# Joining the stages of a three-stage attention kernel early, loading its shifted rows in 112 and 15 partitions, and storing from ScalarE's queue

## What is computed

```python
xn = layernorm(x)                       # x: (16, 512, 128), 16 batches
x = x + causal_attention(xn) + transformer(xn)
# causal_attention: 16 heads of 64, with a relative bias
# transformer, DEPTH = 2 layers, 8 heads of 64, window 64, HID = 341:
h = shift_token(x)                      # columns 64..127 come from the token before
q, k, v = split(h @ wqkv); q, k = rotary(l2norm(q) * qs, l2norm(k) * ksc)
x = x + local_attention(q, k, v) @ wo
h = layernorm(shift_token(x)) * lg + lb
a, g = split(h @ w1 + b1)
x = x + (a * gelu(g)) @ w2 + b2
```

## Time and profile before

| what | us |
|---|---|
| median of 3 runs (2702.74 to 2705.8) | 2703.7 |
| the profiled execution | 2707.02 |
| its span, first to last instruction | 2705.2 |
| causal attention, then 20 us of loading | to 1315.5 |
| local attention, layer 0 / 1 | 1339.0 to 1865.7 / 2018.0 to 2541.8 |
| gated MLP, layer 0 / 1 | 1865.7 to 2010.2 / 2541.8 to 2685.7 |
| sum and store | 2685.7 to 2705.2 |
| PE / ACT / DVE / POOL busy, share of the span | 94% / 80% / 74% / 60% |

### The profile page before, as it was taken

The page is one execution under the profiler, slowest core; times in us unless marked ns, Lnnn a source line. Parts: engine busy times, 40 slices in busy tenths (PEclk is TensorE's granted clock), DMA queues, the critical chain, the costliest instruction groups (busy, mean ns, idle before and its releaser), DMA issues. The chain is left out here.

```text
span 2705.2 us, 71234 instructions
## 1 busy us (share of the span) xinstructions
PE 2547.8 (94%) x24208; PEld 1988.1 (73%) x24208; DVE 2009.4 (74%) x5647; ACT 2158.3 (80%) x6335; POOL 1629.7 (60%) x1947
## 2 busy tenths in 40 slices
PE   7999999999999999999599999997979999999796
PEld 4777777777777777777378888885767888888575
DVE  4666666666666666666389999995659999999565
ACT  5888888888888888888389999996438999999642
POOL 3444444444444444444389999994229999999521
PEclk8999999999999999999799999998989999999898
DMA  2000000000000000000311111111111111111112
GB/s 72 7 7 10 9 9 5 8 7 9 9 9 5 10 7 7 9 6 5 103 41 41 38 42 39 38 42 46 33 26 40 38 42 42 38 40 42 46 33 79
DMA packets 128513, 77.07 MB, mean 28 GB/s; under 512 B 80196, under 2 KB 110736, under 8 KB 128144
## 3 DMA queue, kind: packets, MB, share of 16 engines
q1 hardware_dynamic: 127968, 72.34, 10.9%
q10 hardware_dynamic: 176, 0.07, 0.0%
HBM read 17.58 MB, written 8.41 MB: 10 GB/s over the span
## 5 line engine op out<-in xcount | busy, mean ns | idle before, releaser
L306 POOL TENSOR_SCALAR L<-L,rinv 128x128 f32<-128x128 f32 (+3 forms) x1024 | 522.4, 533 | 622.7 <-DVE rinv L488 622.7
L370 ACT ACTIVATE L<-L,nmax 128x384 f32<-128x384 f32 (+3 forms) x1024 | 571.8, 561 | 144.2 <-DVE nmax L474 144.2
L474 DVE CUSTOM_DVE_ANT_0 L<-bank,bias_tab 128x256 f32<-128x256 f32 (+3 forms) x1024 | 470.5, 479 | 180.3 <-PE bank L590 178.3
L886 ACT ACTIVATE f_L<-bank,f_nmax,f_rn 128x128 f32<-128x128 f32 x1024 | 459.9, 486 | 5.0 <-DVE f_nmax L1013 5.0
L863 POOL TENSOR_TENSOR f_rn<-f_ssq,f_mhalf 128x16 f32<-128x16 f32 x128 | 419.1, 3274 | 18.2 <-DVE f_ssq L997 4.7
L845 POOL TENSOR_TENSOR f_qkr<-f_ab 128x256 f32<-128x256 f32 x512 | 414.3, 838 | 10.3 <-DVE f_ab L964 10.3
L611 PE MATMUL bank<-ident,L 128*128 128x128 f32 x2560 | 370.4, 276 | 2.3 <-DVE PT L215 2.0
L611 PEld LDWEIGHTS bank<-ident,L 128*128 128x128 f32 x2560 | 296.8, 141 | 83.4 <-issue 46.1
L964 DVE TENSOR_TENSOR f_ab<-bank,f_tab 128x512 f32<-128x512 f32 x512 | 347.8, 680 | 8.8 <-ACT f_sq L876 8.8
L632 PE MATMUL bank<-PT,v 128*64 128x512 f32 (+3 forms) x2048 | 303.9, 439 | 0.6 <-DVE yacc L507 0.4
L632 PEld LDWEIGHTS bank<-PT,v 128*64 128x64 f32 x2048 | 126.8, 136 | 166.2 <-issue 164.9
(11 more groups left out here) (145 smaller groups left out, 6390.8 us busy)
## 6 DMA issues: line engine op xcount, KB each, us to landing
f_vm<-f_v SPq DMA_DIRECT2D x224, 128.0 KB, 2.4
f_hs<-xf SPq DMA_DIRECT2D x132, 32.0 KB
f_hs<-xf SPq DMA_DIRECT2D x132, 31.8 KB
xb<-in_L_attn_x SPq DMA_DIRECT2D x16, 256.0 KB, 2.8
out<-yacc SPq DMA_DIRECT2D x32, 128.0 KB, 1.8
f_hs<-xf SPq DMA_DIRECT2D x32, 128.0 KB
out<-f_acc SPq DMA_DIRECT2D x4, 1024.0 KB, 7.5
f_hs<-xf SPq DMA_DIRECT2D x32, 127.0 KB
```

Of the source, the lines that this page charges most:

```text
L306: nc.gpsimd.tensor_scalar(t, t, rinv[:, h % RING, a, i:i + 1], 1.0, ALU.mult, ALU.mult).then_inc(s_N, 1)
L370: nc.scalar.activation(t, t, ACT.Exp, bias=nmax[:, ep % RING, a, i:i + 1], scale=-1.0, accum_out=rsum[:, ep % RING, a, i:i + 1]).then_inc( ...
L474: nc.vector.tensor_tensor_reduce(out=L[:, p % RING, a, LOFF[i]:LOFF[i] + (i + 1) * P], in0=ps_s[a][i], in1=bias_tab[:, 2 * p + a, T - (i + ...
L886: nc.scalar.activation(L[:, ot % 2, a, k, :], ps_s[a][:, k * P:k * P + P], ACT.Exp, bias=nmax[:, ot % 2, a, k:k + 1], scale=rn[:, ot % 2, ...
```

## The change

The change does the following.
- **Causal attention, slots with p == 4:** ScalarE copies `v` before `exps(2, 1)` and does `xT_high` right behind `exps(2, 1)`; VectorE does `xT_low` ahead of the addition to `yacc`.
- **Joins.** The two layers are written out instead of looped. What the local attention needs first (masks, shifted rows of batch 0, rope tables and weights) is built and loaded during the causal attention of batches 0, 1 and 15 (GpSimd, `build_masks`, `prepare_attention`), in layer 1 during the MLP. The weights lie in the memory of the causal stage's bias table. The MLP's rows of batches 0 and 1 are loaded during the attention, and statistics, scale, normalisation, transposes, affine step and low half of batch 0 stand in the attention's last slots (`batch_statistics` and the other `batch_` functions, whose bodies are those that stood in `gated_mlp`).
- **Rows.** Every shifted copy of 127 partitions is now one of 112 and one of 15. In the MLP, for batches from 2 on, the whole rows are copied shifted, and ScalarE writes the unshifted half over them from `xf` (`batch_own_half`). There are four buffers instead of two, and SyncE waits for `hn` of batch `b-4`.
- **MLP order.** PE does two of the three hidden chunks first, then the transposes, the second product and the third chunk; VectorE gates chunk 1 before it adds the second product.
- **End.** `acc` is read back at batch 6 of layer 0's attention. GpSimd adds `xf` to it batch by batch in the last MLP, VectorE adds the second product to that sum, and ScalarE's queue stores each batch four slots later.

The core of the diff:

```diff
+SHIFTED = ((1, 113), (113, P))
...
-        wk_hi, wk_lo = sb("wk_hi", [P, HD], F32R), sb("wk_lo", [P, HD], F32R)
-        wv_hi, wv_lo = sb("wv_hi", [P, HD], F32R), sb("wv_lo", [P, HD], F32R)
+        wk_hi, wk_lo = c["wk_hi"], sb("wk_lo", [P, HD], F32R)
+        wv_hi, wv_lo = c["wv_hi"], c["wv_lo"]
...
-        bias_tab = sb("bias_tab", [P, H, T])
+        bias_tab = w["rows"]
...
+                if b == B - 1:
+                    sp.wait_ge(s_L, at(b, 8 * HP, 8 * 4))
+                    for part in range(3):
+                        load_attention_weights(sp, c, d, w, 0, part, w["s_load"])
+                if b == 1:
+                    sp.wait_ge(s_xf, 1)
+                    sp.wait_ge(w["s_hs_zero"], 1)
+                    for t in range(TT):
+                        load_shifted(sp, c["hs"], xf, 0, t, w["attn"][f"hs{t}"])
...
+                if (b, p) == (0, 6):
+                    build_masks(nc, pool, c, w)
+                for n in {(B - 1, 6): (0, 1, 2), (B - 1, 7): (3, 4, 5), (B, 0): (6, 7)}.get((b, p), ()):
+                    if n == 4:
+                        pool.wait_ge(s_V, HP * B)
+                    if n == 6:
+                        pool.wait_ge(s_k, HP * B)
+                    prepare_attention(nc, pool, c, w, n, w["s_load"])
...
                 fills(1)
+                if p == 4 and item is not None:
+                    value_out(item)
                 exps(2, 1)
-                if item is not None:
+                if p == 4 and has_scores(b) and has_next(b):
+                    xT_high(b + 1, 1 - par)
+                if p != 4 and item is not None:
                     value_out(item)
                 exps(0, 1)
...
                 fills(3)
-                if p == 4 and has_scores(b) and has_next(b):
...
+                if p == 4 and has_scores(b) and has_next(b):
+                    xT_low(b + 1, 1 - par)
...
                                             ALU.add).then_inc(s_Ya, 1)
-                if p == 4 and has_scores(b) and has_next(b):
-                    xT_low(b + 1, 1 - par)
                 logits(0, 0)
...
-    sp.dma_start(hs[1:P, t, half:D], x_t[0:P - 1, half:D]).then_inc(s_hs, 16)
+    for lo, hi in SHIFTED:
+        sp.dma_start(hs[lo:hi, t, half:D], x_t[lo - 1:hi - 1, half:D]).then_inc(s_hs, 16)
...
-def load_shifted_batch(sp, hs, xf, b, r, s_hs):
-    x_b = xf[:, bass.ds(b * TT, TT), :]
+def load_shifted_batch(sp, w, xf, b):
+    hs, s_hs = w["shifted"][b % 4], w["mlp"][f"hs{b % 4}"]
+    x_b = xf[:, b * TT:b * TT + TT, :]
     half = D // 2
-    sp.dma_start(hs[:, r, :, 0:half], x_b[:, :, 0:half]).then_inc(s_hs, 16)
-    sp.dma_start(hs[1:P, r, :, half:D], x_b[0:P - 1, :, half:D]).then_inc(s_hs, 16)
-    sp.dma_start(hs[0:1, r, 1:TT, half:D], x_b[P - 1:P, 0:TT - 1, half:D]).then_inc(s_hs, 16)
+    if b < 2:
+        sp.dma_start(hs[:, :, 0:half], x_b[:, :, 0:half]).then_inc(s_hs, 16)
+        for lo, hi in SHIFTED:
+            sp.dma_start(hs[lo:hi, :, half:D], x_b[lo - 1:hi - 1, :, half:D]).then_inc(s_hs, 16)
+    else:
+        for lo, hi in SHIFTED:
+            sp.dma_start(hs[lo:hi, :, :], x_b[lo - 1:hi - 1, :, :]).then_inc(s_hs, 16)
+    sp.dma_start(hs[0:1, 1:TT, half:D], x_b[P - 1:P, 0:TT - 1, half:D]).then_inc(s_hs, 16)
+def batch_rows_count(b):
+    return 48 * (b // 4 + 1) + (16 if b % 4 < 2 else 0)
+def batch_own_half(nc, act, w, xf, b):
+    half = D // 2
+    act.wait_ge(w["mlp"][f"hs{b % 4}"], batch_rows_count(b))
+    nc.scalar.activation(w["shifted"][b % 4][:, :, 0:half], xf[:, b * TT:b * TT + TT, 0:half],
+                         ACT.Copy).then_inc(w["mlp"]["half"], 1)
...
+def load_attention_weights(eng, c, d, w, l, part, s):
+    if part == 0:
+        eng.dma_start(w["tab"], d["rope"].rearrange("(t p) k e -> p t k e", p=P)).then_inc(s, 16)
+    elif part == 1:
+        eng.dma_start(w["w_raw"], d["wqkv"][l]).then_inc(s, 16)
+    else:
+        eng.dma_start(c["wo4"][:], d["wo"][l].rearrange("(c p) n -> p c n", p=P)).then_inc(s, 16)
...
+def prepare_attention(nc, pool, c, w, n, s_loaded):
+    sem, tab = w["attn"], w["tab"]
+    if n == 0:
+        pool.wait_ge(s_loaded, 16 * 5)
+    if n < 4:
+        nc.gpsimd.tensor_tensor(tab[:, :, n, :], tab[:, :, n, :],
+                                c["qk_scale"][:, n // 2, :].unsqueeze(1).to_broadcast([P, TT, DH]),
+                                ALU.mult).then_inc(sem["tab"], 1)
+    else:
+        some, t = ((0, 2), (2, 3))[(n - 4) // 2], w["w_two"][(n - 4) // 2]
+        raw = w["w_raw"][:, some[0] * FI:some[1] * FI]
+        if n % 2 == 0:
+            nc.gpsimd.tensor_copy(t[0], raw).then_inc(sem["w_hi"], 1)
+        else:
+            pool.wait_ge(sem["w_hi"], (n - 3) // 2)
+            nc.gpsimd.tensor_tensor(t[1], raw, t[0].bitcast(F32), ALU.subtract).then_inc(sem["w_lo"], 1)
...
+            if b in (4, 5) and t == 0:
+                sp.wait_ge(w["s_fill"], 4)
+                sp.wait_ge(sem["x_out"], 2 * TT)
+                load_shifted_batch(sp, w, xf, b - 4)
+            if (l, b, t) == (0, 6, 0):
+                sp.dma_start(w["acc"][:], d["out"].rearrange("b (t p) d -> p (b t) d", p=P)).then_inc(w["s_acc"], 16)
         tile_slots(sp, slot, lag=2)
-        sp.wait_ge(sem["x_out"], 2 * TT)
...
+            if (b, t) == (B, 1):
+                batch_scale(nc, pool, w, 0)
+            if (b, t) == (B, 2):
+                pool.wait_ge(sem["weights"], 16 * 12)
+                nc.gpsimd.tensor_copy(w["w1_hi"][:], c["w1"][:]).then_inc(w["mlp"]["w_hi"], 1)
+                pool.wait_ge(w["mlp"]["w_hi"], 1)
+                nc.gpsimd.tensor_tensor(w["w1_lo"][:], c["w1"][:], w["w1_hi"][:].bitcast(F32),
+                                        ALU.subtract).then_inc(w["mlp"]["w_lo"], 1)
+            if (b, t) == (B + 1, 0):
+                batch_low(nc, pool, w, 0)
...
+            if (b, t) == (B + 1, 0):
+                act.wait_ge(sem["weights"], 16 * 12)
+                batch_affine(nc, act, c, w, 0)
...
-        nc.vector.tensor_copy(w_hi[:], c["wqkv"][:]).then_inc(sem["w_hi"], 1)
-        dve.wait_ge(sem["w_hi"], 1)
-        nc.vector.tensor_tensor(w_lo[:], c["wqkv"][:], w_hi[:].bitcast(F32), ALU.subtract).then_inc(sem["w_lo"], 1)
...
+            if (b, t) == (B, 0):
+                batch_statistics(nc, dve, w, 0)
+            if (b, t) == (B, 2):
+                batch_normalise(nc, dve, w, 0)
+                batch_statistics(nc, dve, w, 1)
...
+            if (b, t) == (B, 3):
+                batch_transposes(nc, pe, c, w, 0)
...
+        nxt = l + 1 if l < DEPTH - 1 else None
+        sp.wait_ge(w["s_zero"], 2 * l + 2)
         def slot(b, r):
-            if isinstance(b, int) and (b < 2 or b >= B):
-                return
-            sp.wait_ge(sem["hn"], at(b, TT, -TT))
-            load_shifted_batch(sp, hs, xf, b, r, sem[f"hs{r}"])
+            if 2 <= b < B:
+                sp.wait_ge(sem["hn"], at(b, TT, -3 * TT))
+                load_shifted_batch(sp, w, xf, b)
+            if nxt is not None and 4 <= b < 7:
+                load_attention_weights(sp, c, d, w, nxt, b - 4, sem["weights"])
+            if nxt is not None and 7 <= b < 11:
+                sp.wait_ge(sem["x_out"], 1)
+                load_shifted(sp, c["hs"], xf, 0, b - 7, w["attn"][f"hs{b - 7}"])
         batch_slots(sp, slot, 0)
...
+        if nxt is None:
+            sp.wait_ge(w["s_stored"], 16 * B)
...
+            if one is not None and one > 0:
+                batch_low(nc, pool, w, one)
+            if now is not None and b > 0:
+                batch_scale(nc, pool, w, b)
+            if l < DEPTH - 1 and 7 <= b < 15:
+                prepare_attention(nc, pool, c, w, b - 7, sem["weights"])
+            if l == DEPTH - 1 and now is not None:
+                pool.wait_ge(w["s_acc"], 16)
+                a = w["acc"][:, b * TT:b * TT + TT, :]
...
+            four = batch_back(b, 4)
+            if l == DEPTH - 1 and four is not None:
+                act.wait_ge(sem["x_out"], four + 1)
+                act.dma_start(d["out"].rearrange("b (t p) d -> p (b t) d", p=P)[:, four * TT:four * TT + TT, :],
+                              w["acc"][:, four * TT:four * TT + TT, :]).then_inc(w["s_stored"], 16)
...
+            if 2 <= b + 1 < B:
+                batch_own_half(nc, act, w, xf, b + 1)
...
+            if now is not None and b > 1:
+                batch_statistics(nc, dve, w, b)
+            gated(1)
             if three is not None:
                 dve.wait_ge(sem["y_done"], at(three, 1, 1))
-                a = xf[:, bass.ds(three * TT, TT), :]
+                if l == DEPTH - 1:
+                    dve.wait_ge(sem["acc"], three + 1)
+                a = (w["acc"] if l == DEPTH - 1 else xf)[:, three * TT:three * TT + TT, :]
                 nc.vector.tensor_tensor(a, ps_y[:].rearrange("p (t d) -> p t d", d=D), a, ALU.add).then_inc(sem["x_out"], 1)
...
             hidden(0)
+            if two is not None:
+                pe.wait_ge(sem["H"], at(two, 3, -1))
```

(9 more changed lines are left out.)

328 lines of the change are left out of this document (154 added, 174 removed).

## The result

The changed kernel takes 2640.6 us (median of 4 runs, 2639.3 to 2641.5) where the kernel before takes 2704.8 (4 runs, 2702.7 to 2706.7): a ratio of 0.9762, 95% interval 0.9746 to 0.9779. The gain is 64.1 us; I had forecast 88.2, and 2616 with a range of 2600 to 2640. The profiled execution has a span of 2639.3 us, 65.9 less than before, so 22.3 of the forecast are missing. I look for them stage by stage, between events that both traces have.

What follows compares the result with a forecast made beforehand. PE was taken to bound the causal stage and SyncE's issue of a 127-partition transfer the MLP, joins being latency; 9 + 21.7 + 16.9 + 17.3 + 7.4 + 15.9 = 88.2 us off 2703.7 gave 2616, range 2600 to 2640.

Steps and rivals of the forecast that it cites:

- So I cost it at nothing.: Mid attention of layer 0: reading `acc` back costs 0 us, up to 17.5 if the transfer is in the way.
- The sign I had set for it, a wait for `vm`: Layer 0's attention: a wait for `vm` showing behind the read-back of `acc` would prove the prediction wrong.
- so I add 2 us to its end.: Attention's drain into the MLP, twice: statistics, normalisation and transposes laid there lengthen it by 2 us (bounds 0 and 4).
- the joins' 9.0 each: Attention into MLP, in each layer: the first hidden product comes 9.0 us earlier.
- The rival of new waits: A join or behind `acc`: tiles stall or drains lengthen by more than 2; about 15 us, 2631; chance 0.11.
- The causal slots: Causal slots with p == 4, 15 times: PE's wait for `xT_lo` shrinks, 9 us gained.
- The way into layer 0: Causal stage into layer 0's attention: the first `hT_lo` comes 21.7 us earlier (19 to 26).
- The slots of the MLP: MLP slots: SyncE falls out of the path and PE's own work bounds a slot at 7.3 us instead of 8.03.
- The MLP's total gain: First hidden product to the MLP's last addition: 7.9 us gained in layer 0, 8.3 in layer 1.
- the long first step: MLP's first step: takes 10.3 us, as GpSimd clears the attention's semaphores before the scale of batch 1.
- Join and end: Into layer 1's attention 7.4 us less (6 to 8); behind the last addition 15.9 less (14 to 17).
- The rival of slots near 8: MLP slots stay near 8 through slow transfers or the longer chain: price 20 us, 2636; chance 0.14.

Runs made afterwards that it cites:

- the first two experiments: The changed kernel with the 4 MB read-back of `acc` cut into 16 transfers of 256 KB, 2628.0 us; or left whole but issued by ScalarE, 2627.8 us.
- the eighth run: Changed kernel with read-back in 16 pieces and the attention's end reordered (VectorE's normalisation and statistics later, PE's transposes and ScalarE's affine step earlier): 2618.9 us.
- the first run: The changed kernel with the 4 MB read-back of `acc` cut into 16 transfers of 256 KB, one per batch of layer 0's attention: 2628.0 us.
- the seventh run: The kernel before, with only its transfers of 127 partitions each split into 112 and 15, in MLP and attention: 2682.8 us.
- the sixth: The changed kernel with the MLP's rows copied as half rows for all batches, split kept, and no write by ScalarE: 2638.9 us.
- the fifth run: The changed kernel with the MLP's whole rows moved in one transfer of 127 partitions instead of 112 and 15: 2750.5 us (one run).

## Why the prediction was wrong, and where it was right

**Wrong: "So I cost it at nothing."** The step on the read-back of `acc` had the mechanism in its text (it fills the queue, and rows wait behind it) and mis-sized the room: I took three slots, some 23 us, from `vm` and set the shifted rows "about as far ahead". They are asked for one slot ahead: 8.4 us from issue to need, where the queue was held for 14.08. The upper bound I gave, 17.5, held the measured 12.9; the value taken was the wrong end. It is shown by the first two experiments, each of which gives it back (12.7 and 12.8 us). The sign I had set for it, a wait for `vm`, never showed: the wait is for the shifted rows.

**Wrong in size: "so I add 2 us to its end."** The drains grew by 6.2 and 6.3, beyond my bound of 4, which cost 3.8 and 4.4 of the joins' 9.0 each. I had said that order counts and then priced the sum of some short operations. What stood there was a queue position ahead of the last multiply, 3.71 us of normalisation that lasts 1.11 alone, and PE's low clock behind the wait. Reordering gave back 9.1 us, shown by the eighth run (6.2 and 4.6 in the two joins of its trace, part of the 6.2 being the clock, which falls early in the first run's drain and not in this one); how much of it is each of its four moves wasn't tried apart.

The stretch itself moves by up to 2.2 us from trace to trace, so the 3.8 and 4.4 are no sharper than that.

These two are 12.9 and 8.2 of the missing 22.3. A further 2.3 are attention slots of 7.855 us instead of 7.835, and the other stretches together gave 1.0 more than forecast. PE has no wait in the slots in either trace, and why they are longer stays open. The rival of new waits had both mechanisms, a stall behind `acc` and drains longer by more than 2, at about 15 us; together they cost 21.

**Right.** The causal slots (8.1 for 9; the 0.6 above is the last slot). The way into layer 0 (21.9 for 21.7). The slots of the MLP: 7.27 for 7.3, by PE's own work, with transposes, affine step and low half beside it. The MLP's total gain (8.4 and 7.5 for 7.9 and 8.3) is partly luck. The 131.1 us run from the first hidden product, not from the first addition, to the last addition. The sum had whole slots in 15 steps before and 14 after, but between the 16 additions only 12 steps are whole ones: these take 96.6 us before and 87.9 after in layer 0, 8.7 less, where 14 steps were priced at 10.2. The last three take 18.95 and 19.3. Against that, the long first step, priced at a loss of 2.3, cost nothing in layer 0 and 0.8 in layer 1: from the first hidden product to the first addition it is 15.6 us in both kernels, and 15.6 and 16.4. Step by step, PE's first took 9.3 and 8.6 us for 10.3, though layer 1's second took 8.9. Join and end: 8.5 for 7.4, 16.8 for 15.9. The Trainium skill, "ScalarE: Activation LUTs", section "What ACT_TABLE_LOAD costs", has 2.66 us for a table switch with its drain. The trace does not agree: in the changed kernel ScalarE's row before the load ends 0.02 us ahead of the 1.28, and its gelu starts 0.01 behind it, in both layers. ScalarE was never held by its stores: the issue takes 0.38 us.

**What it did not separate.** The term for the MLP's slots rested on the transfer alone, and rightly: by the seventh run the split in 112 and 15 makes all of the steady slot's gain, and by the sixth whole rows and ScalarE's half add nothing. The rival of slots near 8 had slow transfers as its mechanism; the fifth run shows that it is real, with 127 partitions only.

## What to carry to other kernels

A large transfer is not hidden because its data is needed late: here what was issued next on its queue was held for 14.08 us of the 18.5 that 4 MB took to land. Put it in pieces (256 KB held nothing here), or on a queue with nothing urgent, and measure the room as the time from the issue of the next small transfer to its use. When work is laid into another stage's drain, find on each engine the last operation that PE waits for and put the new work behind it. Compare drains whose granted clock has the same course, or a change of 1 or 2 us is lost in it. And split a transfer of 127 partitions: 112 and 15 alone gave 24 us here.

## What the hardware showed unexpectedly

- SyncE's queue took 256 KB in runs of 512 B without holding the next issue (0.58 us), held it for 2.03 behind 1 MB and for 14.08 behind 4 MB. With the 4 MB on ScalarE's queue SyncE issued in 0.6 us, and its small transfers landed in time.
- One transfer of 127 partitions moved 18 GB/s in rows of 256 B and 25 in rows of 2 KB (fifth run).
- Four `TENSOR_SCALAR` of 128x128 in SBUF take 1.11 us alone, 1.83 beside a GpSimd multiply of 1.07, 2.42 beside the last 1.6 us of its subtraction, and 3.71 beside its multiply, cast and subtraction in a row; `BATCH_NORM_STATS2` kept its 0.86. The Trainium skill, "SBUF — State Buffer", section "SBUF: two separate sides", has VectorE and GpSimd share a pair of ports under an exclusive lock; the rows agree, and a lock held for a whole GpSimd operation fits the 1.18 us of a `TENSOR_SCALAR` that takes 0.17.
- A PE wait costs more than its length: 9.94 us of wait made 12.85, with the clock at 0.50 for 6.3 us behind it.
- The same instructions at the same place run at either level of the clock: in drains with one order the clock fell 18 us behind the last `hT_lo` or did not, with PE busy 3.7 of 4 us in both, and with the fall the stretch was 0.9 to 2.2 us longer.
